# Linear attention, 32 heads: the sums of y for the output projection move from GpSimd to VectorE, behind each head's gate

## The chip, the cores and the metric

One core of one Trainium2 chip runs the whole kernel. The metric is the time of one execution on the device in microseconds (us), lower is better. TensorE (PE) multiplies matrices, VectorE (DVE) and ScalarE (ACT) do elementwise work on SBUF and PSUM, GpSimd (POOL) does elementwise work on SBUF, and SyncE (SP) issues the transfers.

## What is computed

```python
x  = hidden_states                       # 4 x 256 tokens, 512 wide, fp32
qkv = silu(x @ qkv_w.T)                  # 32 heads, q, k, v of 128 each
# per head, over blocks of 32 tokens:
#   scores = (q k^T) * diag_decay;  out = scores v + (q * q_decay) kv
#   kv = kv * block_decay + (k * k_decay)^T v
attn = rms_norm(out over all 4096 columns) * norm_w
y    = sigmoid(x @ gate_w.T) * attn
x    = layernorm(x + y @ out_w.T)
x    = layernorm(x + x @ base_W.T + base_b + lora(x, router(x)))
```

## The kernel before, in words

The attention is not run block by block: the decay table `dec` turns it into one masked product of the scores of a sequence of 256 tokens. All inputs are fp32. A product is made of three fp32r products, of a rounded part ("hi") and a rest ("lo"): ScalarE writes hi, VectorE subtracts and writes lo (`minus`, L1199, so nearly all of these subtractions show as L1201), and PE multiplies hi·hi, hi·lo and lo·hi (L2032 to L2034).

Large products go by Strassen's scheme in Winograd's form: seven products of half size in place of eight, with sums of blocks ahead of them. The sums of weights are made on GpSimd (`sums`, L1896), those of x once at the start. The input of the output projection is y, four heads by 1024 tokens, and its sums are the matter of this change: `y_sums(g, k)` (L1913) makes three differences for head pair k, and `y_last_sum(g)` (L1927) one more over both. Each is read by `operand_hi` (ScalarE) and `operand_lo` (VectorE), which make the hi and lo operands number 5, 6, 7 and 3 of the output projection.

The heads go in 8 groups of 4. Within a group the stages are `qk0`, `v0`, `v1`, `output`, `g01`, `qk1`, `g23`, `qk2`, `qk3`; group 0 has another start, and the stages `qk0` to `output` exist for groups 1 to 7. Each engine has its own order of these stages, written out by hand, and the engines wait for each other through semaphores alone (`wait_ge(semaphore, count)`). Nothing is reordered at run time: an instruction that is late makes everything behind it on its engine late, unless that would have waited anyway.

The order on VectorE around the change: `qk0` (L1408) ends its work on head h-2 with `gated(h-2, 1)` and goes on with `mask_sum`, `c22_add`, `mask` of head h-1, one half of the value weights (`sums_lo(g,"va","B")`), `c12_add`, `values_lo`, `scores_lo`, `sums_lo(g,"vb","B")`. Then `v0` (L1427) runs `q0_low`, `mask_sum`, `k1_low`, `mask`, `k0_low`, `q1_low`, `scores_lo(h-1,1)`, `add_part`, `c22_add`, `gated(h-1,0)`, `c12_add`, and `v1` (L1441) begins with `add_part(h-1,1)`, `gated(h-1,1)`, `sums_lo(g,"oa","A")`, `mask_sum(h,0)`, `mask(h,0)`.

Masking takes three steps for each head and half: ScalarE copies a strip of scores out of PSUM (`scores_apart`, L616), VectorE adds it back (`mask_sum`) and multiplies by the decay (`mask`). ScalarE then rounds the result (`scores_hi`, L622), VectorE writes the rest (`scores_lo`), and PE multiplies by v (`attention`, L2132).

ScalarE's `u2_copy` (L491) and `u3_copy` (L506) carry a partial result from one PSUM bank to the next. PE's products 6 and 7 of a stage (`p6`, L2094, and `p7`, L2103) wait for them. On ScalarE they stand behind `scores_hi`: in `qk0` and `v0` the order is `scores_hi(h-1,0)`, `k1_out`, then `u2_copy`, and later `q1_out`, `p5_copy`, `u3_copy`, `scale_rows(g,"oa")`, `scores_hi(h-1,1)`. In `v1` it is `square(h-1,1)`, `sums_hi`, `v21_out`, `scores_apart(h,0)`, `p5_copy`, `operand_hi(g,5)`, `scores_hi(h,0)`, `u3_copy`.

GpSimd before: `sums(g,"vb")`, `add_squares(h-2,0)`, `y_sums(g,0)`, `add_squares(h-2,1)`, `sums(g,"oa")`, `add_squares(h-1,0)`, `y_sums(g,1)`, `sums(g,"ob")`, `y_last_sum(g)`, `add_squares(h-1,1)` (L1957). `sums(g,"ob")` needs ScalarE's `scale_rows(g,"ob")` first.

Of the kernel before, what the change touches and what calls it, by code (L numbers as in the profile page):

```python
# [20 lines left out]
HG = 4  # L21
# [46 lines left out]
OUT_SUMS = 8  # L68
# [14 lines left out]
def load_no(g, name):  # L83

    if g == 0:
        return LOADS0.index(name)
    return len(LOADS0) + (g - 1) * len(LOADS) + LOADS.index(name)
# [39 lines left out]
def operand_no(g, i):  # L127

    return 7 * (g - 1) + OUT_ORDER.index(i) + 1
# [21 lines left out]
def build(nc, stream, xt, x, decay, norm_w, base_b, lora_router, router_b, expert_map, ident_in, ones_in, fresh_in, out):  # L151
    ctx = ExitStack()
    with ctx:
# [3 lines left out]
        def sem(name):  # L157
            return ctx.enter_context(nc.semaphore(name))
# [21 lines left out]
        y_temp = y_home[:, :, :]  # L180
# [49 lines left out]
        y11, y12, y21, y22 = y[:, 0:2, W:TOK], y[:, 2:4, W:TOK], y[:, 0:2, 0:W], y[:, 2:4, 0:W]  # L230
# [43 lines left out]
        y_done, y_sum, y_hi, y_lo = sem("y_done"), sem("y_sum"), sem("y_hi"), sem("y_lo")  # L274
# [923 lines left out]
        def _(dve):  # L1198
# [4 lines left out]
            def sums_lo(g, name, part):  # L1203
                m = load_no(g, name)
                dve.wait_ge(t_hi, part_no(g, name, part))
                u0, u1 = (0, 3) if part == "A" else (3, 7)
                runs = pieces(g, name, u0, u1)
                for i, (slot, before, n) in enumerate(runs):
                    ins = minus(wl[:, slot:slot + n, :], stage[:, m % 2, u0 + before:u0 + before + n, :],
                                wh[:, slot:slot + n, :])  # L1210
                    if i == len(runs) - 1:
                        ins.then_inc(t_lo, 1)
# [20 lines left out]
            def c12_add(n):  # L1233
                dve.wait_ge(p_done[3], n + 1)
                dve.wait_ge(cp5, n + 1)
                dve.wait_ge(c12_out, n)
                dve.wait_ge(k0_lo, heads_before(n))
                if n == block_no(GROUPS - 1, QK3):
                    dve.wait_ge(gate_done, 3)
                nc.vector.tensor_tensor(c12_pre, ps[:, B1, :], p5s, ALU.add).then_inc(c12_added, 1)  # L1240
# [34 lines left out]
            def mask_sum(h, e):  # L1275

                dve.wait_ge(s_apart, 2 * h + e + 1)
                nc.vector.tensor_tensor(att_banks(e, SEQ, SC), att_banks(e, SEQ, SC), ssum[:, :, :], ALU.add)\
                    .then_inc(s_parts, 1)
# [10 lines left out]
            def gated(h, e):  # L1290
                dve.wait_ge(sq_done, 2 * h + e + 1)
                n = block_no(h // HG, G01 if h % HG < 2 else G23)
                if e == 0 and h % HG % 2 == 0:
                    dve.wait_ge(c11_out, n + 1)
                    dve.wait_ge(c21_out, n + 1)
                    dve.wait_ge(c12_out, n + 1)
                    dve.wait_ge(c22_out, n + 1)
                dst = by_batch(y[:, h % HG, half(e)])
                nc.vector.scalar_tensor_tensor(out=dst, in0=dst, scalar=1.0, in1=att_banks(e, 0, SEQ),
                                               op0=ALU.add, op1=ALU.mult).then_inc(y_done, 1)  # L1300

            def operand_lo(g, i):

                dve.wait_ge(y_hi, operand_no(g, i))
                hi, lo = y_operand[i]
                if i in (1, 2, 4):
                    ins = nc.vector.scalar_tensor_tensor(out=lo, in0=y_full[i], scalar=-1.0, in1=f32(hi),
                                                         op0=ALU.mult, op1=ALU.subtract)
                else:
                    ins = minus(lo, y_full[i], hi)  # L1310
                ins.then_inc(y_lo, 1)
# [96 lines left out]
            def qk0(g):  # L1408
                n, h = block_no(g, QK0), HG * g
                k0_low(n - 1, h - 1)  # L1410
                add_part(h - 2, 0)
                q1_low(n - 1, h - 1)
                gated(h - 2, 0)
                k1_low(n - 1, h - 1)
                sums_lo(g, "vb", "A")
                add_part(h - 2, 1)
                gated(h - 2, 1)
                mask_sum(h - 1, 0)
                c22_add(n)
                mask(h - 1, 0)  # L1420
                sums_lo(g, "va", "B")
                c12_add(n)
                values_lo(h - 1)
                scores_lo(h - 1, 0)
                sums_lo(g, "vb", "B")

            def v0(g):  # L1427
                n, h = block_no(g, V0), HG * g
                q0_low(n - 1, h)
                mask_sum(h - 1, 1)  # L1430
                k1_low(n - 1, h)
                mask(h - 1, 1)
                k0_low(n - 1, h)
                q1_low(n - 1, h)
                scores_lo(h - 1, 1)
                add_part(h - 1, 0)
                c22_add(n)
                gated(h - 1, 0)
                c12_add(n)

            def v1(g):  # L1441
                n, h = block_no(g, V1), HG * g
# [15 lines left out]
            def output(g):  # L1458
                h = HG * g
                sums_lo(g, "oa", "B")  # L1460
                sums_lo(g, "ob", "B")
                operand_lo(g, 7)
                operand_lo(g, 2)
                out_add(g, "p5", 0)
                out_add(g, "c11", 0)
                out_add(g, "p5", 1)
                out_add(g, "c11", 1)
                operand_lo(g, 3)
                out_add(g, "c22", 0)
                operand_lo(g, 4)  # L1470
                out_add(g, "c22", 1)
                sums_lo(g, "g01", "A")
                out_add(g, "c12", 0)
                sums_lo(g, "g01", "B")
                out_add(g, "c12", 1)
                values_lo(h)
                out_add(g, "c21", 0)
                out_add(g, "c21", 1)
# [386 lines left out]
        def _(pool):  # L1865
# [44 lines left out]
                nc.gpsimd.tensor_tensor(stage[:, s, 6, :], stage[:, s, 2, :], stage[:, s, 3, :], ALU.add)\  # L1910
                    .then_inc(t_sum, 1)

            def y_sums(g, k):  # L1913

                h = HG * g
                made = OUT_SUMS * (g - 1) + 3 * k
                pool.wait_ge(y_done, 2 * (h - 2 + k) + 1)
                if k == 0 and g > 1:
                    pool.wait_ge(y_lo, operand_no(g - 1, 3))
                nc.gpsimd.tensor_tensor(y_temp[:, k, :], y21[:, k, :], y22[:, k, :], ALU.subtract).then_inc(y_sum, 1)  # L1920
                nc.gpsimd.tensor_tensor(y21[:, k, :], y21[:, k, :], y11[:, k, :], ALU.subtract).then_inc(y_sum, 1)
                pool.wait_ge(y_sum, made + 2)
                if k == 0:
                    pool.wait_ge(y_lo, operand_no(g, 1))
                nc.gpsimd.tensor_tensor(y11[:, k, :], y11[:, k, :], y_temp[:, k, :], ALU.subtract).then_inc(y_sum, 1)

            def y_last_sum(g):  # L1927

                h = HG * g
                pool.wait_ge(y_sum, OUT_SUMS * (g - 1) + 6)  # L1930
                pool.wait_ge(y_done, 2 * (h - 1) + 2)
                pool.wait_ge(y_lo, operand_no(g, 5))
                for k in range(2):
                    nc.gpsimd.tensor_tensor(y_temp[:, k, :], y12[:, k, :], y11[:, k, :], ALU.subtract).then_inc(y_sum, 1)

            def next_sums(g, name):
                if g + 1 < GROUPS:
                    sums(g + 1, name)
# [18 lines left out]
            for g in range(GROUPS):  # L1957
                h = HG * g
                if g > 0:
                    sums(g, "vb")  # L1960
                    add_squares(h - 2, 0)
                    y_sums(g, 0)
                    add_squares(h - 2, 1)
                    sums(g, "oa")
                    add_squares(h - 1, 0)
                    y_sums(g, 1)
                    sums(g, "ob")
                    y_last_sum(g)
                    add_squares(h - 1, 1)
                    sums(g, "g01")  # L1970
                sums(g, "qk1")
                sums(g, "g23")
                if g == GROUPS - 1:
                    add_squares(h, 0)
                    sums(g, "qk2")
                    add_squares(h, 1)
                    sums(g, "qk3")
                    for hh in range(h + 1, HEADS):
                        add_squares(hh, 0)
                        add_squares(hh, 1)  # L1980
                    continue
                sums(g, "qk2")
                add_squares(h, 0)
                sums(g, "qk3")
                add_squares(h, 1)
                next_sums(g, "qk0")
                add_squares(h + 1, 0)
                next_sums(g, "va")
                add_squares(h + 1, 1)
# [672 lines left out]
```

## Time and profile before

| | |
|---|---|
| median of 3 runs | 993.08 us (992.87 to 993.71) |
| profiled execution | 994.48 us |
| its span, first to last instruction | 992.7 us |
| PE busy | 982.8 us (99%) |
| PE weight load busy (beside PE) | 862.8 us (87%) |
| DVE busy | 799.5 us (81%) |
| ACT busy | 727.6 us (73%) |
| POOL busy | 458.3 us (46%) |
| granted TensorE clock, mean | 0.999 |

The profile is of one execution. Busy time of an engine is the time in which one of its instructions ran; successive instructions overlap a little, so that the distance from one start to the next is some 0.08 us shorter than a duration on DVE. Matmuls are pipelined too: those of 256 columns start 0.12 us apart and those of 512 columns 0.23 us apart, though the profile gives them longer durations. A row's bracket, as `[1.60 <-ACT sq L471]`, is the time for which the engine sat idle ahead of it and what released it. Times in a timeline count from the start of the span.

### The profile page before, as it was taken

What the parts mean: (1) busy time and instruction counts of PE and PEld (TensorE: products, weight loads), DVE (VectorE), ACT (ScalarE), POOL (GpSimd) and SP (SyncE); (2) the same over time, 40 slices, a digit from 0 to 9 for tenths busy, and PEclk for the clock granted to TensorE, in tenths of its full rate; (3) what the DMA queues carried; (4) which work ended last, traced back from release to release, by engine and by line L of the source; (5) the groups of instructions that cost most, each with busy time, mean ns of one, the idle gap of its engine ahead of it and who ended that gap; (6) DMA issues with size and microseconds to landing.
All of it is one profiled execution on the core that took longest, in us unless ns stands there. A gap on an engine that the chain in (4) does not pass through costs nothing.

```text
span 992.7 us, 15943 instructions
## 1 busy us (share of the span) xinstructions
PE 982.8 (99%) x5569; PEld 862.8 (87%) x5569; DVE 799.5 (81%) x1058; ACT 727.6 (73%) x1261; POOL 458.3 (46%) x426
## 2 busy tenths in 40 slices
PE   9999999999999999999999999999999999999997
PEld 7888998889888898889988898888988899888896
DVE  6667887878867889679877788778886788889877
ACT  6678885788767885788857887577867888587653
POOL 1353464346544463434653465444635345531423
PEclk9999999999999999999999999999999999999999
DMA  6021211211121012212111111210122121110402
GB/s 212 29 64 36 75 37 57 58 44 52 51 65 51 30 52 72 65 35 75 35 58 58 44 52 51 65 51 30 52 71 64 33 78 35 59 52 22 160 12 86
DMA packets 52800, 57.79 MB, mean 58 GB/s; under 512 B 4336, under 2 KB 47728, under 8 KB 52720
## 3 DMA queue, kind: packets, MB, share of 16 engines
q1 hardware_dynamic: 52720, 56.77, 18.3%
q8 instruction: 45, 0.74, 0.3%
q14 instruction: 35, 0.29, 0.1%
HBM read 54.65 MB, written 2.10 MB: 57 GB/s over the span
## 4 chain that ended last, share of the span: by engine, by line
PE 92%; DVE 2%; ACT 2%; issue 1%; DMA 1%; POOL 1%; SPq 0%; POOLq 0%; ACTq 0%; DVEq 0%
PE ps L2032 24%; PE ps L2033 24%; PE ps L2034 23%; PE ps L2026 3%; PE ps L2028 3%; PE ps L2027 3%; PE ps L2129 2%; PE ps L2123 2%; PE ps L2125 2%; PE ps L2124 2%; PE ps L2143 1%; DMA stage<-stream 1%; DVE wl L1201 1%; PE ps L2127 1%; PE ps L2145 1%
## 5 line engine op out<-in xcount | busy, mean ns | idle before, releaser
L1903 POOL TENSOR_TENSOR stage<-stage 128x512 f32<-128x512 f32 x75 | 106.2, 1416 | 352.6 <-DMA stage<-stream 289.7
L2032 PE MATMUL ps<-xh,wh 128*128 128x512 f32 x658 | 260.4, 396 | 1.4 <-ACT stg L517 1.0
L2033 PE MATMUL ps<-xl,wh 128*128 128x512 f32 x658 | 257.1, 391 | 0.0
L2034 PE MATMUL ps<-xh,wl 128*128 128x512 f32 x658 | 256.2, 389 | 0.0
L1201 DVE TENSOR_TENSOR wl<-stage,wh 128x768 fp32r<-128x768 f32 (+3 forms) x183 | 202.6, 1123 | 23.2 <-ACT wh L471 22.1
L471 ACT ACTIVATE wh<-stage 128x768 fp32r<-128x768 f32 (+3 forms) x183 | 147.6, 834 | 12.8 <-POOL stage L1910 6.9
L2032 PEld LDWEIGHTS ps<-xh,wh 128*128 128x128 f32 x658 | 123.7, 188 | 26.7 <-ACT ps L471 2.1
L2034 PEld LDWEIGHTS ps<-xh,wl 128*128 128x128 f32 x658 | 123.6, 188 | 26.7
L2033 PEld LDWEIGHTS ps<-xl,wh 128*128 128x128 f32 x658 | 123.7, 188 | 21.8
L1946 POOL TENSOR_TENSOR sqacc<-sqacc,sq 128x512 f32<-128x512 f32 x64 | 90.6, 1416 | 108.8 <-ACT sq L635 108.8
L471 ACT ACTIVATE ps<-ps 128x512 f32<-128x512 f32 x150 | 87.4, 586 | 52.5 <-PE ps L2034 43.2
L2032 PE MATMUL ps<-wh,xh 128*128 128x256 f32 (+1 forms) x423 | 122.6, 290 | 0.0
L2034 PE MATMUL ps<-wh,xl 128*128 128x256 f32 (+1 forms) x423 | 121.7, 288 | 0.0
L2033 PE MATMUL ps<-wl,xh 128*128 128x256 f32 (+1 forms) x423 | 121.5, 287 | 0.0
L1910 POOL TENSOR_TENSOR stage<-stage 128x256 f32<-128x256 f32 x75 | 80.2, 1069 | 5.9
L2033 PEld LDWEIGHTS ps<-wl,xh 128*128 128x128 f32 x423 | 80.9, 191 | 0.3
L2032 PEld LDWEIGHTS ps<-wh,xh 128*128 128x128 f32 x423 | 80.9, 191 | 0.3
L2034 PEld LDWEIGHTS ps<-wh,xl 128*128 128x128 f32 x423 | 80.8, 191 | 0.0
L1906 POOL TENSOR_TENSOR stage<-stage 128x256 f32<-128x256 f32 x75 | 74.0, 987 | 5.9
L1201 DVE TENSOR_TENSOR s<-ps,s 128x768 fp32r<-128x768 f32 x64 | 60.9, 952 | 19.2 <-ACT s L471 19.1
L471 ACT ACTIVATE s<-ps 128x768 fp32r<-128x768 f32 x64 | 51.7, 808 | 16.4 <-DVE ps L1271 16.4
L1271 DVE TENSOR_TENSOR ps<-ps,dec 128x768 f32<-128x768 f32 x64 | 61.5, 961 | 1.2
(224 smaller groups left out, 2322.2 us busy)
## 6 DMA issues: line engine op xcount, KB each, us to landing
stage<-stream SPq DMA_DIRECT2D x75, 384.0 KB, 3.4
stage<-stream SPq DMA_DIRECT2D x79, 128.0 KB, 2.1
dec<-decay SPq DMA_DIRECT2D x32, 192.0 KB, 2.5
stage<-stream SPq DMA_DIRECT2D x13, 256.0 KB, 3.2
acc<-xt SPq DMA_DIRECT2D x8, 256.0 KB, 5.9
v<-x SPq DMA_DIRECT2D x8, 256.0 KB, 6.1
out<-v SPq DMA_DIRECT2D x8, 256.0 KB, 2.1
y_home<-lora_router SPq DMA_DIRECT2D x1, 512.0 KB, 5.0
```

The source lines that it names most:

```text
L471: return nc.scalar.activation(dst, src, ACT.Copy, **kw)
L1201: return nc.vector.tensor_tensor(dst, full, f32(hi), ALU.subtract)
L1271: nc.vector.tensor_tensor(att_banks(e, 0, SC), att_banks(e, 0, SC), dec[:, h % 2, :].unsqueeze(1).broadcast_to([P, 2, SC]), ALU.mult)\
L1903: nc.gpsimd.tensor_tensor(stage[:, s, 1:5:3, :], stage[:, s, 0:6:5, :], stage[:, s, 7:8, :].broadcast_to([P, 2, U]), ALU.add).then_inc(t_p ...
L1906: nc.gpsimd.tensor_tensor(stage[:, s, 2, :], stage[:, s, 1, :], stage[:, s, 5, :], ALU.add)\
L1910: nc.gpsimd.tensor_tensor(stage[:, s, 6, :], stage[:, s, 2, :], stage[:, s, 3, :], ALU.add)\
L1946: nc.gpsimd.tensor_tensor(sqacc[:, e, :], sqacc[:, e, :], sq[:, :], ALU.add).then_inc(sq_added, 1)
L2026: nc.tensor.matmul(dst, wt[0], mv_[0], start=start, stop=False)
L2027: nc.tensor.matmul(dst, wt[0], mv_[1], start=False, stop=False)
L2032: nc.tensor.matmul(dst, wt[0], mv_[0], start=start, stop=False, skip_group_check=True)
L2033: nc.tensor.matmul(dst, wt[0], mv_[1], start=False, stop=False, skip_group_check=True)
L2034: return nc.tensor.matmul(dst, wt[1], mv_[0], start=False, stop=stop, skip_group_check=True)
```

## The change: what it does

The three differences of `y_sums` and the last one of `y_last_sum` are issued by VectorE instead of GpSimd. `y_sums(g, 0)` stands behind `gated(h-2, 1)` in `qk0`, `y_sums(g, 1)` behind `c12_add` at the end of `v0`, and `y_last_sum(g)` in `output` between the two weight splits `sums_lo(g,"oa","B")` and `sums_lo(g,"ob","B")`. The last sum is one instruction of 1024 columns in place of two of 512. The waits of the functions are the same, on the other engine. GpSimd's other work keeps its order.

```diff
--- before.py
+++ after.py
@@ -1299,6 +1299,28 @@
                 nc.vector.scalar_tensor_tensor(out=dst, in0=dst, scalar=1.0, in1=att_banks(e, 0, SEQ),
                                                op0=ALU.add, op1=ALU.mult).then_inc(y_done, 1)
 
+            def y_sums(g, k):
+
+                h = HG * g
+                made = OUT_SUMS * (g - 1) + 3 * k
+                dve.wait_ge(y_done, 2 * (h - 2 + k) + 1)
+                if k == 0 and g > 1:
+                    dve.wait_ge(y_lo, operand_no(g - 1, 3))
+                nc.vector.tensor_tensor(y_temp[:, k, :], y21[:, k, :], y22[:, k, :], ALU.subtract).then_inc(y_sum, 1)
+                nc.vector.tensor_tensor(y21[:, k, :], y21[:, k, :], y11[:, k, :], ALU.subtract).then_inc(y_sum, 1)
+                dve.wait_ge(y_sum, made + 2)
+                if k == 0:
+                    dve.wait_ge(y_lo, operand_no(g, 1))
+                nc.vector.tensor_tensor(y11[:, k, :], y11[:, k, :], y_temp[:, k, :], ALU.subtract).then_inc(y_sum, 1)
+
+            def y_last_sum(g):
+
+                h = HG * g
+                dve.wait_ge(y_sum, OUT_SUMS * (g - 1) + 6)
+                dve.wait_ge(y_done, 2 * (h - 1) + 2)
+                dve.wait_ge(y_lo, operand_no(g, 5))
+                nc.vector.tensor_tensor(y_temp, y12, y11, ALU.subtract).then_inc(y_sum, 2)
+
             def operand_lo(g, i):
 
                 dve.wait_ge(y_hi, operand_no(g, i))
@@ -1415,6 +1437,7 @@
                 sums_lo(g, "vb", "A")
                 add_part(h - 2, 1)
                 gated(h - 2, 1)
+                y_sums(g, 0)
                 mask_sum(h - 1, 0)
                 c22_add(n)
                 mask(h - 1, 0)
@@ -1437,6 +1460,7 @@
                 c22_add(n)
                 gated(h - 1, 0)
                 c12_add(n)
+                y_sums(g, 1)
 
             def v1(g):
                 n, h = block_no(g, V1), HG * g
@@ -1458,6 +1482,7 @@
             def output(g):
                 h = HG * g
                 sums_lo(g, "oa", "B")
+                y_last_sum(g)
                 sums_lo(g, "ob", "B")
                 operand_lo(g, 7)
                 operand_lo(g, 2)
@@ -1910,29 +1935,6 @@
                 nc.gpsimd.tensor_tensor(stage[:, s, 6, :], stage[:, s, 2, :], stage[:, s, 3, :], ALU.add)\
                     .then_inc(t_sum, 1)
 
-            def y_sums(g, k):
-
-                h = HG * g
-                made = OUT_SUMS * (g - 1) + 3 * k
-                pool.wait_ge(y_done, 2 * (h - 2 + k) + 1)
-                if k == 0 and g > 1:
-                    pool.wait_ge(y_lo, operand_no(g - 1, 3))
-                nc.gpsimd.tensor_tensor(y_temp[:, k, :], y21[:, k, :], y22[:, k, :], ALU.subtract).then_inc(y_sum, 1)
-                nc.gpsimd.tensor_tensor(y21[:, k, :], y21[:, k, :], y11[:, k, :], ALU.subtract).then_inc(y_sum, 1)
-                pool.wait_ge(y_sum, made + 2)
-                if k == 0:
-                    pool.wait_ge(y_lo, operand_no(g, 1))
-                nc.gpsimd.tensor_tensor(y11[:, k, :], y11[:, k, :], y_temp[:, k, :], ALU.subtract).then_inc(y_sum, 1)
-
-            def y_last_sum(g):
-
-                h = HG * g
-                pool.wait_ge(y_sum, OUT_SUMS * (g - 1) + 6)
-                pool.wait_ge(y_done, 2 * (h - 1) + 2)
-                pool.wait_ge(y_lo, operand_no(g, 5))
-                for k in range(2):
-                    nc.gpsimd.tensor_tensor(y_temp[:, k, :], y12[:, k, :], y11[:, k, :], ALU.subtract).then_inc(y_sum, 1)
-
             def next_sums(g, name):
                 if g + 1 < GROUPS:
                     sums(g + 1, name)
@@ -1959,13 +1961,10 @@
                 if g > 0:
                     sums(g, "vb")
                     add_squares(h - 2, 0)
-                    y_sums(g, 0)
                     add_squares(h - 2, 1)
                     sums(g, "oa")
                     add_squares(h - 1, 0)
-                    y_sums(g, 1)
                     sums(g, "ob")
-                    y_last_sum(g)
                     add_squares(h - 1, 1)
                     sums(g, "g01")
                 sums(g, "qk1")
```

## Rows read from the trace of the kernel before

**Rows 1.** The page, busy time of each engine over the span

```profile
PE 982.8 (99%) x5569; PEld 862.8 (87%) x5569; DVE 799.5 (81%) x1058; ACT 727.6 (73%) x1261; POOL 458.3 (46%) x426
```

**Rows 2.** Waits of PE: engine, line, released by, us in total, times, longest

```profile
PE ps L2384 <- DVE s L1667: 1.4, 1, 1.4
PE ps L2032 <- ACT stg L517: 1.0, 2, 0.6
```

**Rows 3.** Groups of instructions by line: form, count, busy us, mean ns, idle before

```profile
L1921 POOL TENSOR_TENSOR y<-y 128x512 f32<-128x512 f32 x14 | 22.8, 1631 | 0.0
...
L1934 POOL TENSOR_TENSOR y_home<-y 128x512 f32<-128x512 f32 x14 | 17.9, 1303 | 1.3 <-DVE vl L1201 1.3
```

**Rows 4.** Timeline of VectorE, group 3: start, duration, line, operands, idle before

```profile
338.49 1.28 DVE L1201 TENSOR_TENSOR k<-stg,k 128x512 fp32r<-128x512 f32 x1
339.70 2.05 DVE L1201 TENSOR_TENSOR wl<-stage,wh 128x768 fp32r<-128x768 f32 x1
...
342.77 0.69 DVE L1299 SCALAR_TENSOR_TENSOR y<-y,ps 128x512 f32<-128x512 f32 x1 [0.67 <-ACT sq L635]
343.37 0.42 DVE L1278 TENSOR_TENSOR ps<-ps,ssum 128x256 f32<-128x256 f32 x1
...
344.30 0.96 DVE L1271 TENSOR_TENSOR ps<-ps,dec 128x768 f32<-128x768 f32 x1
345.17 1.51 DVE L1201 TENSOR_TENSOR wl<-stage,wh 128x256 fp32r<-128x256 f32 x2
```

**Rows 5.** Timeline of GpSimd, same stretch

```profile
337.93 1.29 POOL L1946 TENSOR_TENSOR sqacc<-sqacc,sq 128x512 f32<-128x512 f32 x1 [1.58 <-ACT sq L635]
...
344.24 1.29 POOL L1946 TENSOR_TENSOR sqacc<-sqacc,sq 128x512 f32<-128x512 f32 x1
```

**Rows 6.** Timeline of ScalarE, same stretch

```profile
345.57 0.82 ACT L471 ACTIVATE s<-ps 128x768 fp32r<-128x768 f32 x1
...
347.48 0.58 ACT L471 ACTIVATE ps<-ps 128x512 f32<-128x512 f32 x1
```

**Rows 7.** Timeline of TensorE, first matmuls of three steps

```profile
349.84 0.28 PE L2032 MATMUL ps<-wh,xh 128*128 128x256 f32 x1
...
356.77 0.28 PE L2026 MATMUL ps<-s,vh 128*128 128x256 f32 x1
...
367.49 0.28 PE L2032 MATMUL ps<-wh,xh 128*128 128x256 f32 x1
```

**Rows 8.** Timeline of VectorE, later in group 3

```profile
352.74 0.67 DVE L1201 TENSOR_TENSOR k<-stg,k 128x512 fp32r<-128x512 f32 x1
...
354.97 0.96 DVE L1201 TENSOR_TENSOR s<-ps,s 128x768 fp32r<-128x768 f32 x1 [0.95 <-ACT s L471]
...
357.54 0.68 DVE L1240 TENSOR_TENSOR stg<-ps,stg 128x512 f32<-128x512 f32 x1
359.83 0.43 DVE L1287 TENSOR_TENSOR ps<-ps,sq 128x256 f32<-128x256 f32 x1 [1.60 <-ACT sq L471]
...
361.66 1.59 DVE L1201 TENSOR_TENSOR wl<-stage,wh 128x768 fp32r<-128x768 f32 x1
```

**Rows 9.** Timeline of GpSimd, later in group 3

```profile
357.27 1.29 POOL L1946 TENSOR_TENSOR sqacc<-sqacc,sq 128x512 f32<-128x512 f32 x1
...
362.40 2.01 POOL L1903 TENSOR_TENSOR stage<-stage 128x512 f32<-128x512 f32 x1
```

**Rows 10.** Timeline of ScalarE, later in group 3

```profile
356.79 1.70 ACT L471 ACTIVATE stage<-stage,nw 128x256 f32<-128x256 f32 x4
...
363.64 0.60 ACT L471 ACTIVATE stg<-ps 128x512 f32<-128x512 f32 x1 [1.05 <-PE ps L2034]
...
365.77 0.60 ACT L471 ACTIVATE ps<-ps 128x512 f32<-128x512 f32 x1
```

**Rows 11.** Timeline of VectorE, output stage of group 3

```profile
377.63 1.21 DVE L1307 SCALAR_TENSOR_TENSOR yl<-y,yh 128x1024 fp32r<-128x1024 f32 x1
```

**Rows 12.** Timeline of TensorE, output stage of group 3

```profile
380.00 0.39 PE L2032 MATMUL ps<-yh,wh 128*128 128x512 f32 x1
```

## The prediction

> **What bounds the kernel now.** I read the page first. PE is busy for 982.8 of 992.7 us, VectorE for 799.5 (81%), and GpSimd for 458.3 (46%) [rows 1]. The waits of PE say the same more strictly: its longest is 1.4 us at the start, the next 1.0 us in two pieces, and no row names a wait for VectorE in the middle of the kernel that is above 0.2 us [rows 2]. So PE is fed without holes, a stall of PE anywhere is added to the end, and there is next to nothing for a change on other engines to win. GpSimd's sums of y wait for nothing that costs, and nobody is listed as waiting for them; 14 instructions per line, of 1303 to 1631 ns each [rows 3]. The question is therefore only how much lateness each helper may take on before PE feels it. For that the averages are no use, and I went through the timelines of group 3 engine by engine, noting where PE starts a product and when what it needs was done. Groups 1 to 7 repeat with a period of about 116 us. Six of them agree within about 0.1 us at the places below; group 6 has tighter places at its start.
>
> **Three margins of PE in group 3.** `p6` of stage `v0` starts at 349.84 [rows 7]; its `u2_copy` ends at 347.48 + 0.58 = 348.06 [rows 6]: margin 1.78 us. `attention(h-1,1)` starts at 356.77 [rows 7]; its `scores_lo` ends at 354.97 + 0.96 = 355.93 [rows 8]: margin 0.84. `p7` of `v1` starts at 367.49 [rows 7]; its `u3_copy` ends at 365.77 + 0.60 = 366.37 [rows 10]: margin 1.12. Of each some 0.05 is the way of a semaphore (the smallest distance that I find between such an end and the start that it releases).
>
> **What is added to VectorE.** A difference of two SBUF operands of 512 columns takes 0.67 us when nothing disturbs it, and the next instruction starts some 0.60 after its start: the row at 352.74 stands for `y_sums` [rows 8]. The last sum of 1024 columns takes 1.21, spacing 1.13 [rows 11] (the row is of the same shape). A group gets 6 x 0.60 + 1.13 = 4.7 us, seven groups 33 us; VectorE would be at 832 us or 84%. On average that fits. In place it does not, because the queue is dense there.
>
> **What is taken from GpSimd, and the lock.** Four lines of 14 instructions go, about 80 us in all ([rows 3] show the largest and the smallest). Nobody waits for them, so this is worth nothing directly. But VectorE and GpSimd hold each other up: `k1_low` at 338.49 took 1.28 instead of 0.67, and it ended 0.55 after GpSimd's `add_squares` ended (337.93 + 1.29 = 339.22) [rows 4, 5]. The split at 339.70 took 2.05, beside a sum of y on GpSimd, where the same form takes 0.95 alone [rows 4]. Instructions of VectorE with a PSUM operand, such as the mask at 344.30, keep their 0.96 beside GpSimd [rows 4]. I take this as: of a VectorE instruction with two SBUF inputs and a GpSimd instruction, the second waits for the end of the first. The Trainium skill (SBUF — State Buffer, "SBUF: two separate sides") says this outright: the pair of ports is an exclusive lock, taken for a whole instruction by whichever starts first. The trace agrees with it in the 0.55 us above. By that rule the added instructions, all with two SBUF inputs, queue behind GpSimd; without it they would not, and the sum would be that of the second rival below.
>
> **First insertion, `y_sums(g,0)` in `qk0`.** It starts where `mask_sum` did, at 343.37, behind `gated` at 342.77 [rows 4]. That start does not move: `gated` waited 0.67 for ScalarE's square [rows 4], so the relief at 339.70 is lost in idle time. The square ends at 342.73, so GpSimd, now idle, starts its `add_squares` at 342.81 instead of 344.24 [rows 5] and ends at 344.10. The first difference waits for that and ends near 344.67 (1.3 us), the second near 345.25, the third must see the second done and starts at 345.30. `mask_sum` starts at 345.90, 2.53 late. The mask (344.30, end 345.26) ends at 347.79. ScalarE's `scores_hi`, which started at 345.57, starts at 347.82: 2.25 late [rows 4, 6]. What follows on ScalarE is back to back, so `u2_copy` ends at 350.31, and `p6` starts at 350.36: 0.52 lost.
>
> On VectorE the two pieces at 345.17 no longer meet `add_squares` and take 0.24 less (0.41 for the first in place of 0.65), so the queue is 2.53 - 0.24 = 2.29 late. It has no idle time up to 354.02, and the 0.95 ahead of 354.97 is a wait for ScalarE [rows 8], whose own chain (`q1_out`, `u3_copy`, `scale_rows`, `scores_hi`) hangs on VectorE's `q0_low` and is 2.29 late too. So `scores_lo` ends at 355.93 + 2.29 = 358.22, and `attention(h-1,1)` starts at 358.26 instead of 356.77. **PE is 1.49 us late here** (0.52 at `p6`, 0.56 at `p7` and 0.41 at the attention; the sum is simply 2.29 less the margin).
>
> **Second insertion, `y_sums(g,1)` at the end of `v0`.** `c12_add` starts at 357.54 + 2.29 = 359.83, so the first difference is issued at 360.43. GpSimd's `add_squares` comes to 359.57 to 360.86 (it was at 357.27 [rows 9], behind `sums(g,"oa")`, which waits for ScalarE). Then comes `sums(g,"ob")`: it was at 362.40 [rows 9] because the sums of y stood ahead of it. Now it needs only `scale_rows`, 356.79 + 1.70 + 2.29 = 360.78 [rows 10]. Its three instructions (1.29, 0.74, 0.74 us undisturbed) alternate with the three differences under the lock: differences end at 361.4, 363.25 and 364.55. `add_part(h-1,1)` starts at 364.5 instead of 359.83 [rows 8], 4.6 late; ScalarE alone would have made it wait to 362.1.
>
> The square and what follows on ScalarE are 4.6 late, less the 1.05 us of idle ahead of 363.64 [rows 10]: 3.5 at `p5_copy`. VectorE gets 0.64 back at 361.66, where 1.59 becomes 0.95, as GpSimd is done by then [rows 8]; the next mask is about 4.0 late, and `scores_hi` and `u3_copy` 3.6. `u3_copy` ends at 369.95 instead of 366.37, `p7` starts at 370.0 instead of 367.49. **PE is 2.5 us late by then**, 1.0 more than before.
>
> **Third insertion, `y_last_sum`.** 1.13 us, at a lateness relative to PE that is gone by then: VectorE has two more idle places of about 0.5 in `v1`, and the split of "ob", once 1.88, runs in 0.95. The operand split at 377.63 ends at 378.84, the product that needs it starts at 380.00 [rows 11, 12]: margin 1.16 against 1.13. I count 0; if something else is late there too, up to 0.5. What `sums` of later stages or the loads do is not late: GpSimd waits for transfers before each of them.
>
> **Sum.** 2.5 us in each of 7 groups: 17.5 us. The profiled execution of 994.48 us (span 992.7) becomes 1012, and the median of 993.08, which lies 1.4 below it, 1010.5. From below the cost of an insertion is 0 (all in idle time). From above it is what the nearest long row says, 2.05 for each of six differences plus 1.2, 13.5 us a group; the dense queue in group 3 makes 2.5 the value that I take.
>
> **Rivals.**
> (1) The differences of `y_sums(g,1)` do not alternate with `sums(g,"ob")`. Then `add_part(h-1,1)` is about 2.5 late and the margin at `p7` holds, since PE is itself 1.49 late: 7 x 1.5 = 10.5, 1003.5 us. For it: the meeting hangs on tenths of a us at 360.8. Against it: `sums(g,"ob")` took 2.01 at 362.40 against 1.29 for the same form elsewhere, beside VectorE's split [rows 8, 9], which is the alternation.
> (2) No lock for these operands. `mask_sum` is 1.88 late, the queue 1.64, and the attention loses 1.64 - 0.84 + 0.04 = 0.84 a group: 999 us. Against it: the 1.28 at 338.49.
> (3) Worse: ScalarE enters `output` 2.5 to 3 late, where the copy for the second product has only 0.24 us of margin; each group loses 0.5 to 1 more: 1014 to 1018 us.
> (4) No change: the 19% of idle time on VectorE takes it all, 993. This is what the page's average says, against the dense timeline. The Trainium skill leans this way (GPSIMD Engine Reference, "Engine selection": elementwise work with two inputs belongs on VectorE, where it is about twice as fast). The trace agrees on the factor (1.30 against 0.67), and no wait in the profile makes that factor worth time.
> (5) Faster: the lock. The sums of y on GpSimd cost VectorE 1.1 us at 339.70, 0.6 at 361.66 and more in `v1`, up to 2.7 a group. If these come back where PE is short, and the additions fall into idle time, the kernel gains at most what PE waits for in the middle of a group. That is a wait on ScalarE's q output at the start of `g23`, 0.4 to 0.6 a group by the timeline: 989 to 992 us. It decides only if the queue in `qk0` has 2 us to spare, which it has not.
>
> **Numbers.** Forecast 0.50, (1) 0.22, (2) 0.10, (3) 0.09, (4) 0.05, (5) 0.04. The range takes in (2) and most of (3): 999 to 1017; outside lie (4), (5), the lower half of (2) and the tail of (3), under 0.2. What can be told from no change is about 0.2%, 2 us: faster 0.04, same 0.05, slower 0.91.
>
> **What would show it.** In the profile after: PE idle ahead of its first matmul of `p6` and of `attention(h-1,1)` in `v0`, and ahead of `p7` in `v1`, released by ScalarE or VectorE, seven times each; about 1.5 us a group up to the attention and 1.0 at `p7`. The first difference should take about 1.3 us and those of `y_sums(g,1)` up to 1.9, the rest 0.67. GpSimd's busy time falls by about 80 us, VectorE's rises by 33 less the relief. I am wrong if PE has no such idle time, if the differences all take 0.67 (then (2)), or if the stalls sit in `output` (then (3)).

## The result, and the profile after

The changed kernel takes 1011.23 us (median of 4 runs, 1010.26 to 1011.51) against 993.38 us in the runs beside it: ratio 1.0171, 95% interval 1.0152 to 1.019. By the ratio it is slower by 17 us (15.1 to 18.9); the two medians lie 17.9 us apart. The forecast was 1010.5 us, 17.4 us above the median before. All costs below are taken from the ratios.

The page of the changed kernel, for the engines shown in [rows 1]: VectorE is busy for 30 us more, GpSimd for 82 us less.

```profile
span 1009.5 us, 15943 instructions
...
PE 987.3 (98%) x5569; PEld 863.2 (86%) x5569; DVE 829.9 (82%) x1107; ACT 726.0 (72%) x1261; POOL 376.4 (37%) x370
```

The busy shares say nothing of 17 us: VectorE's goes from 81% to 82%. The waits of PE do, beside [rows 2] (the two rows there are still in it, with their 1.4 and 1.0 to 1.1 us):

```profile
PE ps L2031 <- ACT ps L471: 10.3, 22, 0.9
PE ps L2025 <- DVE s L1201: 1.8, 7, 0.3
PE ps L2383 <- DVE s L1692: 1.4, 1, 1.4
PE ps L2031 <- ACT stg L517: 1.1, 2, 0.6
```

22 waits for a PSUM copy of ScalarE are three in each of seven groups and one of 0.4 us in group 0, at 59.58; 7 waits for `scores_lo` of VectorE are one in each. The first matmuls of those four places in group 3, on TensorE's timeline (start, duration, line, idle before); they answer to [rows 7]:

```profile
355.10 0.39 PE L2031 MATMUL ps<-wh,xh 128*128 128x256 f32 x1 [0.32 <-ACT ps L471]
...
359.73 0.39 PE L2031 MATMUL ps<-wh,xh 128*128 128x256 f32 x1 [0.32 <-ACT ps L471]
...
363.11 0.35 PE L2025 MATMUL ps<-s,vh 128*128 128x256 f32 x1 [0.25 <-DVE s L1201]
...
374.88 0.39 PE L2031 MATMUL ps<-wh,xh 128*128 128x256 f32 x1 [0.83 <-ACT ps L471]
375.10 0.28 PE L2032 MATMUL ps<-wl,xh 128*128 128x256 f32 x1
```

The bracket understates a stall, because a matmul's modelled end lies beyond the start of the next. The right measure is how far the start of a product moves against the kernel before. Taking the start of every product of both traces, the distance grows in group 3 by 0.48 at `p6` of `v0`, by 0.47 at `p7`, by 0.41 at `attention(h-1,1)` and by 0.99 at `p7` of `v1`, and by another 0.10 behind each of the first, second and fourth and 0.07 behind the third. (After a stall the second matmul too starts 0.22 us behind the first, where 0.12 is usual: 375.10 against 374.88.) That is 2.7 us, and the other six groups give the same within 0.1: 18.7 us in all. In the stages outside `v0` and `v1`, behind the first 12 us of the kernel, the distance moves by 0.5 at most at single places, both ways.

VectorE in `qk0` of the changed kernel, to lay beside [rows 4]; L1309, L1310 and L1314 are the three differences:

```profile
347.50 0.69 DVE L1299 SCALAR_TENSOR_TENSOR y<-y,ps 128x512 f32<-128x512 f32 x1 [1.78 <-ACT sq L635]
348.11 1.29 DVE L1309 TENSOR_TENSOR y_home<-y 128x512 f32<-128x512 f32 x1
349.32 0.68 DVE L1310 TENSOR_TENSOR y<-y 128x512 f32<-128x512 f32 x1
350.04 0.69 DVE L1314 TENSOR_TENSOR y<-y,y_home 128x512 f32<-128x512 f32 x1
350.65 0.42 DVE L1278 TENSOR_TENSOR ps<-ps,ssum 128x256 f32<-128x256 f32 x1
```

`gated` to `mask_sum` is now 3.15 us, where it was 0.60. GpSimd's timeline has `add_squares` at 347.55 for 1.30: the first difference, issued at 348.11, ends 0.55 after it. At the end of `v0` the differences meet `sums(g,"ob")`. VectorE first, then GpSimd, beside [rows 8, 9]:

```profile
365.18 0.96 DVE L1309 TENSOR_TENSOR y_home<-y 128x512 f32<-128x512 f32 x1
366.07 1.78 DVE L1310 TENSOR_TENSOR y<-y 128x512 f32<-128x512 f32 x1
367.88 1.10 DVE L1314 TENSOR_TENSOR y<-y,y_home 128x512 f32<-128x512 f32 x1
368.91 0.42 DVE L1287 TENSOR_TENSOR ps<-ps,sq 128x256 f32<-128x256 f32 x1
...
370.73 1.42 DVE L1201 TENSOR_TENSOR wl<-stage,wh 128x768 fp32r<-128x768 f32 x1
```

```profile
364.31 1.29 POOL L1948 TENSOR_TENSOR sqacc<-sqacc,sq 128x512 f32<-128x512 f32 x1
365.67 1.63 POOL L1928 TENSOR_TENSOR stage<-stage 128x512 f32<-128x512 f32 x1
367.38 1.06 POOL L1931 TENSOR_TENSOR stage<-stage 128x256 f32<-128x256 f32 x1
368.52 1.07 POOL L1935 TENSOR_TENSOR stage<-stage 128x256 f32<-128x256 f32 x1
370.04 1.30 POOL L1948 TENSOR_TENSOR sqacc<-sqacc,sq 128x512 f32<-128x512 f32 x1 [0.45 <-ACT sq L635]
```

The last row of each is the weight split `sums_lo(g,"oa","A")` and the `add_squares(h-1,1)` that it now meets.

The groups of lines give the whole kernel: 14 instructions per line whose undisturbed duration is 0.68, and 7 of the last sum.

```profile
L1310 DVE TENSOR_TENSOR y<-y 128x512 f32<-128x512 f32 x14 | 17.2, 1229 | 0.0
...
L1309 DVE TENSOR_TENSOR y_home<-y 128x512 f32<-128x512 f32 x14 | 15.8, 1131 | 0.0
...
L1314 DVE TENSOR_TENSOR y<-y,y_home 128x512 f32<-128x512 f32 x14 | 12.6, 899 | 0.5
...
L1322 DVE TENSOR_TENSOR y_home<-y 128x1024 f32<-128x1024 f32 x7 | 8.5, 1216 | 0.0
```

These are 54 us, of which VectorE's busy time shows only 30. Comparing both traces instruction by instruction, VectorE's other instructions are 18 us shorter in sum, 10 of them where one ran beside a sum of y on GpSimd in the kernel before. The remaining 6 us are the overlap of successive instructions, which busy time counts once.

### The profile page after: what moved, and what is told of

It is laid out like the page before. It is cut to its first block, busy times and chain, and to the rows that moved or that the text cites. A ratio compares the mean times of both kernels' runs of the same rounds, so it can differ in the third digit from the quotient of the medians.

```text
span 1009.5 us, 15943 instructions
## 1 busy us (share of the span) xinstructions
PE 987.3 (98%) x5569; PEld 863.2 (86%) x5569; DVE 829.9 (82%) x1107; ACT 726.0 (72%) x1261; POOL 376.4 (37%) x370
## 4 chain that ended last, share of the span: by engine, by line
PE 75%; DVE 11%; ACT 5%; issue 5%; DMA 1%; POOL 1%; SPq 0%; DVEq 0%; ACTq 0%; POOLq 0%
PE ps L2031 20%; PE ps L2032 19%; PE ps L2033 19%; PE ps L2025 3%; PE ps L2027 3%; PE ps L2026 3%; DVE wl L1201 2%; DVE y L1310 2%; DVE y_home L1309 2%; PE ps L2128 1%; DVE ps L1271 1%; PE ps L2142 1%; PE ps L2122 1%; PE ps L2124 1%; PE ps L2123 1%
## 5 line engine op out<-in xcount | busy, mean ns | idle before, releaser
L1928 POOL TENSOR_TENSOR stage<-stage 128x512 f32<-128x512 f32 x75 | 109.1, 1455 | 421.3 <-DMA stage<-stream 333.0
L1201 DVE TENSOR_TENSOR wl<-stage,wh 128x768 fp32r<-128x768 f32 (+3 forms) x183 | 187.3, 1038 | 23.7 <-ACT wh L471 22.5
L2031 PE MATMUL ps<-wh,xh 128*128 128x256 f32 (+1 forms) x423 | 124.7, 295 | 10.0 <-ACT ps L471 10.0
L1935 POOL TENSOR_TENSOR stage<-stage 128x256 f32<-128x256 f32 x75 | 79.5, 1060 | 5.9
L1931 POOL TENSOR_TENSOR stage<-stage 128x256 f32<-128x256 f32 x75 | 67.9, 905 | 5.9
```

Source lines behind the costliest of these rows:

```text
L1201: return nc.vector.tensor_tensor(dst, full, f32(hi), ALU.subtract)
L1928: nc.gpsimd.tensor_tensor(stage[:, s, 1:5:3, :], stage[:, s, 0:6:5, :], stage[:, s, 7:8, :].broadcast_to([P, 2, U]), ALU.add).then_inc(t_p ...
L1931: nc.gpsimd.tensor_tensor(stage[:, s, 2, :], stage[:, s, 1, :], stage[:, s, 5, :], ALU.add)\
L2031: nc.tensor.matmul(dst, wt[0], mv_[0], start=start, stop=False, skip_group_check=True)
```

## The experiments

All edits are on the changed kernel; ratios are to the kernel before on the same chip. The theory: what counts is where an instruction stands in VectorE's queue, and whom it meets under the lock. The rival: the cost follows the amount of work added.

**e1.** `y_sums(g, 0)` back on GpSimd, in its old place; VectorE's second set waits for its count.

```diff
                 gated(h - 2, 1)
-                y_sums(g, 0)
                 mask_sum(h - 1, 0)
...
                     add_squares(h - 2, 0)
+                    pool_y_sums(g, 0)
                     add_squares(h - 2, 1)
```

> y_sums(g, 0) goes back to GpSimd, the other two insertions stay on VectorE. Theory (place, dense queue and lock): the 1.5 us a group up to the attention of v0 vanish. y_sums(g, 1) then meets add_squares and sums(ob) as in my chain but from an on-time queue: add_part(h-1,1) 2.4 us late, 1.3 after ScalarE's idle time, against a margin of 1.07 at p7 of v1: 0.3 us a group, 995.5 us (994 to 998). Rival (amount: the cost is shared out by the work added to VectorE, 18 us for 4.7 us a group): 2.9 of 4.7 stay, 1004.4 us.

997.08 us, ratio 1.002 (1.001 to 1.0031), 2 us more than before. PE waits for a PSUM copy of ScalarE seven times: once in group 0, as in the changed kernel, and at `p7` of `v1` in groups 2 to 7 (that of group 1, 0.31 by the starts, is too short for the list). No wait of another kind is new:

```profile
PE ps L2047 <- ACT ps L471: 2.1, 7, 0.6
```

In group 3 the differences start at 359.06, meet `sums(g,"ob")` as they do in the changed kernel, and `add_part` starts at 362.81, 2.1 us after ScalarE's strip was ready (360.73). ScalarE's idle time and the margin take most of that: PE falls back by 0.39 us at `p7` of `v1` and by 0.10 behind it. The other groups give 0.31 to 0.39, group 6 0.79.

**e2.** `y_sums(g, 1)` back on GpSimd, `y_sums(g, 0)` on VectorE (the same edit for the other pair).

> y_sums(g, 1) goes back to GpSimd, y_sums(g, 0) and the last sum stay on VectorE. Theory: PE loses what it lost up to the attention, 1.5 us a group, and nothing at p7 of v1, because VectorE's lateness of 2.3 is taken up by the idle 1.6 ahead of add_part and by PE's own delay: 1004 us (1003 to 1006). Rival (amount): 1004.4 us, the same here, but then e1 must be the same as this one; theory says that e1 and e2 differ by 8 us, and that their costs (2 and 11) do not add up to 18.

1005.53 us, ratio 1.011 (1.0095 to 1.0126), 11 us. The stalls up to the attention of `v0` are all there (0.47, 0.48, 0.41 in group 3), the one at `p7` of `v1` is gone but for 0.29 in group 7:

```profile
PE ps L2046 <- ACT ps L471: 4.4, 15, 0.4
PE ps L2040 <- DVE s L1201: 1.8, 7, 0.3
```

e1 and e2 put the same work back and differ by 9 parts in a thousand, where the rival wants them alike. Their costs, 2 and 11, add up to 13 and not to 17. (By the starts of products the stalls of `v0` cost 1.5 to 1.6 a group in e2 as in the changed kernel; what doesn't add up is the last one, 0.4 to 0.5 in most groups of e1 and none in e2, but 1.1 with both.) The slack of `v1` (ScalarE's idle time and the margin at `p7`) is spent once: either insertion alone has it to itself, with both the second finds it used.

**e3.** Both `y_sums` on GpSimd, only the last sum on VectorE.

> Both y_sums on GpSimd, only y_last_sum on VectorE. Theory: a margin of 1.16 against 1.13, no stall: 993.4 us within 1. Rival (amount): 1.13 of 4.7, 4.3 us: 997.7 us.

993.5 us, ratio 0.9989 (0.998 to 0.9998). The list of PE's waits has no new one in groups 1 to 7. The third term is 0, as worked out; the amount would have cost 4 us.

**e4.** A wait more on GpSimd, nothing else.

```diff
+                    pool.wait_ge(y_sum, OUT_SUMS * (g - 1) + 6)
                     sums(g, "ob")
```

> The changed kernel, and GpSimd's sums(g, ob) wait until y_sums(g, 1) is done, so that the two do not alternate; nothing is taken from VectorE. Theory (lock): the second and third difference take 0.7 us instead of 1.8 and 1.1, add_part(h-1,1) comes 1.5 us earlier relative to the gate, and the 1.1 us a group at p7 of v1 vanish or shrink to 0.3, as the sums of ob now meet the weight split of oa: 1004 us (1003 to 1006). Rival (amount, or no lock): 1011 us or slower, since only a wait is added.

1004.02 us, ratio 1.0093 (1.0076 to 1.011). A kernel with one wait more in it is 7 to 8 us faster than the changed one (7.2 by the medians, 7.7 by the ratios). The second and third difference are undisturbed throughout:

```profile
L1314 DVE TENSOR_TENSOR y<-y,y_home 128x512 f32<-128x512 f32 x14 | 9.7, 692 | 0.5
L1310 DVE TENSOR_TENSOR y<-y 128x512 f32<-128x512 f32 x14 | 9.5, 679 | 0.0
```

**e5** and **e6.** The same for `add_squares(h-2, 1)`, alone and together with the wait of e4.

```diff
+                    pool.wait_ge(y_sum, OUT_SUMS * (g - 1) + 3)
                     add_squares(h - 2, 1)
```

> The changed kernel, and GpSimd's add_squares(h-2, 1) wait until y_sums(g, 0) is done. Theory (lock): the first difference takes 0.68 us instead of 1.29, the queue of qk0 is 1.64 late instead of 2.3, so PE loses no time at p6 and 0.8 to 0.9 instead of 1.5 up to the attention: 5 us less than the changed kernel, 1006 us. Without the lock: 1011 us or slower.

1007.05 us, ratio 1.0128 (1.0114 to 1.0141). In group 3 the stall at `p6` is gone, those at `p7`, the attention and `p7` of `v1` stay (0.47, 0.41, 0.99).

> The changed kernel with both waits on GpSimd: no difference of y meets a GpSimd instruction. Theory: 0.9 us a group up to the attention and little at p7 of v1: 999 to 1001 us, which is the cost of the place alone. Without the lock: 1011 us or slower.

1000.36 us, ratio 1.0058 (1.0045 to 1.0071). So of the 17 us some 11 are the lock: GpSimd instructions met by the differences. About 6 are the place alone, the stalls at `p7` and the attention of `v0`. One meeting is left, against what I expected of e6: the first difference of the second set still stands behind `add_squares(h-1,0)`, which neither wait holds back, and takes 0.96 in group 3 (362.28). It comes behind the stalls of `v0`, and `p7` of `v1` has none in e6, so it costs nothing there. The 14 first differences of e6 beside the 14 second ones:

```profile
L1309 DVE TENSOR_TENSOR y_home<-y 128x512 f32<-128x512 f32 x14 | 11.5, 824 | 0.0
...
L1310 DVE TENSOR_TENSOR y<-y 128x512 f32<-128x512 f32 x14 | 9.5, 682 | 0.0
```

**e7.** `y_sums(g, 0)` one place earlier. Nothing is taken from VectorE.

```diff
                 add_part(h - 2, 1)
-                gated(h - 2, 1)
                 y_sums(g, 0)
+                gated(h - 2, 1)
                 mask_sum(h - 1, 0)
```

> The changed kernel with y_sums(g, 0) one place earlier, ahead of gated(h-2, 1) instead of behind it, all else the same. VectorE idles there for 1.78 us in the changed kernel, waiting for ScalarE's square, and GpSimd is idle too; the three differences need 1.84. Theory: the stalls of v0 vanish, and what stays is that of y_sums(g, 1) from an on-time queue as in e1: 995.5 us (994 to 998). Rival (amount): 1011 us.

993.82 us, ratio 0.9998 (0.9989 to 1.0007). The timeline of VectorE, group 3: the differences sit where `gated` waited for ScalarE's square, take 0.68 each, and `gated` follows without idle time.

```profile
338.46 0.95 DVE L1201 TENSOR_TENSOR wl<-stage,wh 128x768 fp32r<-128x768 f32 x1
339.33 0.42 DVE L1287 TENSOR_TENSOR ps<-ps,sq 128x256 f32<-128x256 f32 x1
339.66 0.68 DVE L1309 TENSOR_TENSOR y_home<-y 128x512 f32<-128x512 f32 x1
340.26 0.68 DVE L1310 TENSOR_TENSOR y<-y 128x512 f32<-128x512 f32 x1
340.98 0.69 DVE L1314 TENSOR_TENSOR y<-y,y_home 128x512 f32<-128x512 f32 x1
341.58 0.68 DVE L1299 SCALAR_TENSOR_TENSOR y<-y,ps 128x512 f32<-128x512 f32 x1
```

The first row is the weight split that took 2.05 at 339.70 [rows 4], beside a sum of y on GpSimd, and takes 0.95 here.

An exchange of two neighbours in the order gives the 17 us back. It comes out just below my range of 994 to 998: PE falls back by 0.1 to 0.2 a group at `p7` of `v1` here, not by the 0.3 to 0.4 of e1. In group 3 the first difference of the second set starts 1.18 us behind PE's start of the attention here, 1.38 in e1. The two traces show where: the two pieces of `sums_lo(g,"va","B")` take 1.53 at 346.07 in e1, beside an `add_squares` that GpSimd, busy with its sums of y, starts only at 345.16; in e7 GpSimd starts it at 341.58, and the two pieces take 1.28. So in e1 the sums of y on GpSimd still disturb VectorE.

**e8.** e7 with the wait of e4.

> As e7, and sums(g, ob) wait for y_sums(g, 1). All 33 us of added work stay on VectorE, in its idle places. Theory: add_part(h-1,1) is 0.5 to 0.9 late, which ScalarE's 1.05 of idle time takes up: 993.5 to 995 us, no slower than the kernel before by more than 0.2%. Rival (amount): 1011 us.

992.84 us, ratio 0.9989 (0.9979 to 0.9999), in 12 runs against 23 of before. The waits of PE are those of before again, but for one of 0.4 us for VectorE, and at none of the four places in `v0` and `v1` does the start of a product move by 0.05 or more. The interval lies below 1, but by less than the 0.2% that I call a difference: equal, at best 1 us faster, with all the added work on VectorE.

```profile
PE ps L2384 <- DVE s L1692: 1.4, 1, 1.4
PE ps L2032 <- ACT stg L517: 1.0, 2, 0.6
PE ps L2209 <- ACT xh L471: 0.7, 1, 0.7
```

**e9.** A try at what PE still waits for: in `qk1` of e8, ScalarE makes q before rounding the values, and VectorE adds c22 and splits q before the values.

```diff
                 part(h, 1)
-                values_hi(h + 1)
                 q0_out(n, h + 1)
+                values_hi(h + 1)
...
                 add_part(h, 1)
-                values_lo(h + 1)
                 c22_add(n)
                 q0_low(n, h + 1)
+                values_lo(h + 1)
                 c12_add(n)
```

> As e8, and in stage qk1 ScalarE makes q_out(h+1) ahead of values_hi(h+1), and VectorE makes c22_add and q0_low ahead of values_lo. The kernel before has few waits of PE left to win: 0.8 us in group 0 and 0.56 in group 3 ahead of the first product of g23 stand behind values_hi on ScalarE. Theory: these two go, 1 to 1.5 us, 991.5 us, just at what can be measured. Rival: the stage is dense too, the swapped order opens a stall in each of 7 groups at c12_add or u2_copy, whose margins there are 0.05 to 0.25: 994 to 998 us.

996.1 us, ratio 1.0016 (1.0007 to 1.0025). Against the kernel before this is within the 0.2% that I call no difference; against e8 (0.9989) it is not, and 991.5 is ruled out. The waits say that the rival was right. The two waits for q are gone from the list, and of the seven for a PSUM copy of ScalarE six are new (the seventh, in group 0 at 59.26, is in e8 too):

```profile
PE ps L2032 <- ACT ps L471: 4.7, 7, 1.0
```

By the starts of products, groups 0 to 6 each have a new stall 4.3 us behind the first product of `g23`, of 0.2 to 1.2 us.

The same count over all runs: at the four places of `v0` and `v1` PE falls back, in seven groups together, by 18.7 us in the changed kernel, 3.7 in e1, 11.4 in e2, 0 in e3, 11.0 in e4, 14.7 in e5, 7.2 in e6, 1.9 in e7 and 0 in e8. The costs by the ratios (17, 2, 11, -1, 9, 13, 6, 0 and -1) follow, 0.4 to 2.1 us below.

## Why the prediction was right

Point by point. The rows of PE give the growth of its lateness in group 3.

| step | predicted | measured |
|---|---|---|
| first difference, behind `add_squares` | 1.3 | 1.29 |
| `mask_sum` later than before, from `gated` | 2.53 | 2.55 |
| PE at `p6` of `v0` | 0.52 | 0.48 + 0.10 |
| PE at `p7` of `v0` | 0.56 | 0.47 + 0.10 |
| PE at `attention(h-1,1)` | 0.41 | 0.41 + 0.07 |
| second set: ends behind its first issue | 1.0, 2.8, 4.1 | 0.96, 2.67, 3.81 |
| weight split of "oa" behind it | 0.95 | 1.42 |
| PE at `p7` of `v1` | 1.0 | 0.99 + 0.10 |
| `output` | 0 | 0 |
| a group | 2.5 | 2.7 |
| GpSimd busy | -80 | -82 |

The lock, which I took from a few rows of the kernel before, holds for the new ones; e4, e5 and e6 show it by taking the meetings away, and e3 that the last sum is free. The place, which I argued from margins, is shown by e7.

Four things were less good. First, I did not know of the 0.10 us that PE needs after a stall. It does not add up over a group, because each later stall ends when its helper is done, however late PE already is: PE is 0.48, 1.05, 1.56 and 2.61 us late at the four places, where I had 0.52, 1.08, 1.49 and 2.51. Only the last 0.10 is added. With 0.10 more of lateness at `p7` of `v1` itself a group comes to 2.7 and not 2.5.

Second, the seven groups give 18.7 us by the starts of products, and the span grew by 16.8. Of the 1.9 between, 0.9 is the part of the kernel ahead of the first of the changed stages, where this execution happened to be quicker. The other 1.0 came back, net, at single places, the largest in the last group (0.46, where PE had waited for a copy of ScalarE in the kernel before) and in `qk0` of group 6 (0.34, where PE had waited behind a split held up by GpSimd's sums of y). So my sum was 1.2 us too small for what it added up, and left out 1.0 us that pulled the other way: that the forecast came within 1 us of the median is in part luck.

Third, two errors in the second insertion cancel. The alternation at the end of `v0` was taken 0.3 us too long: two instructions under the lock overlap by some 0.1 us, and `add_part` is 4.3 us later, not 4.6. But the relief behind it was taken 0.5 too large. I let the weight split that took 1.59 at 361.66 [rows 8] run in 0.95, "as GpSimd is done by then". GpSimd is not: its next `add_squares`, released by the same late square, starts at 370.04, ahead of the split at 370.73, and the split takes 1.42 (1.42 or 1.43 in each of groups 1 to 6, where it shows as one row). The next mask is 4.1 us later in place of 4.0, and the 1.0 at `p7` of `v1` comes out right partly by luck.

Fourth, the price of the faster rival was misread. I gave it 0.4 to 0.6 us a group. The wait list says 1.0 us in two pieces [rows 2], and the timeline shows it in groups 0 and 3 alone. There, counted by the starts of products (0.79 and 0.56), at most 1.4 us could be won, not 3 to 4; and e9 shows that this place is as dense as the others. This touches no number of the forecast.

My rival (1), no alternation, is what e4 builds, and its price (1003.5) is what e4 gives (1004.0). Rival (2), no lock, was given 999; e6, which takes away the meetings that cost anything and leaves the place, gives 1000.4.

## What to carry to other kernels

Where one engine is full and the others hold fixed orders, don't ask whether an engine has 19% of idle time: ask, for each thing that the full engine waits for, how long before its use it was done, and follow the inserted time along the queue until an idle place takes it up. Margins of about 1 us decided here over 17 us, and an exchange of two neighbouring steps gave them back. And slack is spent once: two insertions can cost more than the sum of each alone (17 against 13).

## What the runs showed of the hardware

Here VectorE's `tensor_tensor` with two SBUF inputs and GpSimd's `tensor_tensor` take turns, whole instruction by whole instruction. A difference of 0.68 us took 1.29, 0.96, 1.78 and 1.10 beside GpSimd and 0.68 without, and GpSimd's 0.74 became 1.06. Holding GpSimd back until VectorE is done can therefore be worth more than letting it run: one wait, 7 to 8 us (e4). TensorE's second matmul of 256 columns after a stall started 0.10 us later than usual at `p6` and `p7`, 0.07 at the attention.
